# Two attention layers of one kernel: value products in groups of four blocks in the first, and two late units written one head pair earlier in the second

## What is computed

```python
# layer 0, for each of 16 heads; k and v are repeated over 4 heads
s1 = einsum(q1, k1) * scale + mask;  s2 = einsum(q2, k2) * scale + mask
out = einsum(softmax(s1) - lam * softmax(s2), v)         # then a norm over (tokens, 2*DH), and @ Wo
y = mxfp4(input) @ mxfp4(weight).T + bias
# layer 1, for each of 16 heads
attn = softmax(where(causal, q @ k.T / sqrt(16), -inf));  out = attn @ v;  x = out @ Wo + bo
# experts: sigmoid gate, 4 of 16 experts by groups, and one shared expert
```

## Time and profile before

| | |
|---|---|
| median of 3 runs | 812.24 us (810.98 to 812.34) |
| the profiled execution's own time | 813.73 us |
| its span | 812.0 us |
| PE busy | 761.3 us (94%) |
| DVE busy | 552.4 us (68%) |
| ACT busy | 429.8 us (53%) |
| POOL busy | 367.3 us (45%) |
| value products L771, both layers | 216 us in two forms (162.7 and 53.3) |
| mean granted PE clock | 0.985 of 2.4 GHz |

### The profile page before, as it was taken

The page is one execution under the profiler, slowest core; times in us unless marked ns, Lnnn a source line. Parts: engine busy times, 40 slices in busy tenths (PEclk is TensorE's granted clock), DMA queues, the critical chain, the costliest instruction groups (busy, mean ns, idle before and its releaser), DMA issues. The chain is left out here.

```text
span 812.0 us, 12974 instructions
## 1 busy us (share of the span) xinstructions
PE 761.3 (94%) x3783; PEld 370.6 (46%) x3783; DVE 552.4 (68%) x1408; ACT 429.8 (53%) x922; POOL 367.3 (45%) x706
## 2 busy tenths in 40 slices
PE   4888999999999999998998998999799999999995
PEld 3342222222222322224744232332278888888883
DVE  3778777877777777714874886885077665566666
ACT  2432466666656666673242365776745554455552
POOL 1762565664324433431331132335366665566664
PEclk9999899999999999999999999999999999999998
DMA  6394640020011002101056236453442211122111
GB/s 198 125 285 132 148 114 20 18 66 15 15 45 45 16 16 55 35 22 53 1 174 141 79 92 179 155 175 112 144 102 65 65 65 50 55 64 63 66 69 56
DMA packets 56980, 68.86 MB, mean 85 GB/s; under 512 B 13793, under 2 KB 35714, under 8 KB 56915
## 3 DMA queue, kind: packets, MB, share of 16 engines
q1 hardware_dynamic: 56840, 68.10, 29.2%
q10 hardware_dynamic: 80, 0.07, 0.0%
HBM read 46.37 MB, written 15.44 MB: 76 GB/s over the span
## 5 line engine op out<-in xcount | busy, mean ns | idle before, releaser
L823 ACT ACTIVATE top<-ps 128x512 f32<-128x512 f32 (+3 forms) x384 | 170.7, 491 | 126.7 <-PE ps L751 126.7
L751 PE MATMUL ps<-mid 99*128 99x512 bf16 (+3 forms) x576 | 182.9, 333 | 5.7 <-ACT mid L823 3.4
L865 DVE CUSTOM_DVE_ANT_0 ps<-ps,keep 128x512 f32<-128x512 f32 (+3 forms) x320 | 162.0, 530 | 27.3 <-PE ps L727 27.1
L727 PE MATMUL ps<-mid 96*128 96x512 bf16 (+3 forms) x512 | 167.6, 340 | 5.1 <-PEq L249 1.0
L771 PE MATMUL ps<-top,mid 128*33 128x512 f32 (+3 forms) x768 | 162.7, 503 | 0.0
L1652 PE MATMUL ps<-xp,wp 128*128 128x512 f32 (+1 forms) x600 | 146.3, 394 | 3.2 <-ACT wp L1702 2.7
L751 PEld LDWEIGHTS ps<-mid 99*128 99x128 bf16 x576 | 53.7, 98 | 174.9 <-ACT top L823 103.2
L1652 PEld LDWEIGHTS ps<-xp,wp 128*128 128x128 f32 (+1 forms) x600 | 112.7, 188 | 28.6 <-ACT xp L1704 3.2
L960 POOL TENSOR_SCALAR_AFFINE_SELECT top<-top 128x128 f32<-128x128 f32 x256 | 71.2, 291 | 107.3 <-ACT top L823 105.2
L823 ACT ACTIVATE mid<-ps 128x512 f32<-128x512 f32 (+1 forms) x192 | 82.2, 494 | 58.2 <-PE ps L751 36.0
L869 DVE TENSOR_REDUCE top<-ps 128x1 f32<-128x512 f32 x128 | 88.4, 690 | 32.9 <-PE ps L727 32.6
(11 more groups left out here) (217 smaller groups left out, 851.2 us busy)
## 6 DMA issues: line engine op xcount, KB each, us to landing
mid<-part_scratch SPq DMA_DIRECT2D x9, 1152.0 KB, 8.9
part_scratch<-top SPq DMA_DIRECT2D x18, 384.0 KB, 2.9
cw_s<-combine_rows SPq DMA_DIRECT2D x48, 128.0 KB, 3.0
part_scratch<-top SPq DMA_DIRECT2D x18, 256.0 KB, 3.1
top<-in_w SPq DMA_DIRECT2D x6, 634.0 KB, 5.2
mid<-part_scratch SPq DMA_DIRECT2D x9, 384.0 KB, 4.0
top<-in_w SPq DMA_DIRECT2D x4, 640.0 KB, 7.1
top<-in_w SPq DMA_DIRECT2D x4, 633.0 KB, 6.0
```

The lines of the kernel that those rows point to most:

```text
L727: nc.tensor.matmul(ps[:, s_bank(turn), 0:w], queries(pair, m)[0:PARTS, i * P:(i + 1) * P], keys(pair, m)[0:PARTS, c * 512:c * 512 + w], st ...
L751: nc.tensor.matmul(ps[:, ST_BANK + n % AHEAD, 0:w], keys(pair, m)[0:STACK, j * P:(j + 1) * P], queries(pair, m)[0:STACK, q0:q0 + w], start ...
L823: nc.scalar.activation(pr[:, n % RING, 0:w], ps[:, ST_BANK + n % AHEAD, 0:w], ACT.Exp, scale=0.25).then_inc(p_ready, 1)
L865: ins = nc.vector.tensor_tensor_reduce(bank, bank, msk[:, 512 - w:512], -1.0 if low else 1.0, 3e38 if low else -3e38, ALU.add, ALU.min if ...
```

## The change

```diff
-                RING, LAG = 8, 1
-
-                GROUPS = [(b, b + 2) for b in range(0, 8 if not first else PAIR, 2)]
-                if not first:
-                    GROUPS += [(b, b + 4) for b in range(8, PAIR, 4)]
+                RING, LAG = 9 if first else 8, 1
+
+                GROUPS = [(b, b + 2) for b in range(0, 8, 2)] if not first else [(0, 4), (4, 8)]
+                GROUPS += [(b, b + 4) for b in range(8, PAIR, 4)]
...
                             outputs(sp, pair, 0)
-                            if pair == 1:
-                                unsent(sp, 1)
                             if pair + 1 < N:
                                 late(sp, pair + 1)
+                            if pair == 0:
+                                unsent(sp, 1)
```

## The result

The changed kernel takes 814.16 us (median of 13 runs, 812.72 to 817.44); the kernel before, run between them on the same chip, 812.45 us (13 runs, 810.81 to 813.25). The ratio is 1.0033, 95% interval 1.0022 to 1.0044: 1.8 to 3.6 us slower. The forecast was 813.5 us, within 809.5 to 817, and "within 0.2%" was its likeliest case; the interval of the ratio lies just beyond that.

A forecast was written before the change was run, and what follows sets the result against it. PE's own stream was taken as layer 0's bound. Layer 0: -0.5 - 0.2 + 2.9 = +2.2 us; layer 1: -3.4 + 2.5 = -0.9; sum +1.3, so 812.24 becomes 813.5 us, range 809.5 to 817.

The forecast's parts named there:

- The price of a group and a joint: PE, layer 0 value products: a group costs 0.23 us besides its columns, a joint 0.01 to 0.02; each group saved, 0.21.
- Rival 4: Layer 0: weight loads of joints are exposed, four in about 0.15 us; up to +14 us, 826; chance 0.02.
- The stalls: Layer 0: PE waits 0.36 at k = 13, 0.21 at 5, 0.32 at 21, 0.16 at 1; 1.07 of 1.27 us a pair.
- Rival 2: Layer 0: the groups save their whole 19.7 us and nothing stalls, 791.6; chance 0.05.
- The tail: Layer 0's last 38 blocks: stalls of 5.0 us against ten joints worth 2.1, so 2.9 us lost.
- The body of layer 0: Pairs 1 to 13 of layer 0: joints save slightly more than stalls cost, -0.5 us in all, between -2.6 and +1.
- the failed step: Layer 1: moved writes hold SP until some 481, so `rows(2)` is issued late; 2.5 us of stall ending pair 1.
- The other half of the step: Layer 1: PE has no margin for `rows(2)`, so its 2.5 us of lateness become 2.5 us of stall.
- in time but lands behind the writes, 0.3 to 0.8: Layer 1: if SP isn't held, `rows(2)` is issued in time but lands behind the writes, 0.3 to 0.8 us.
- The -3.4 for the two waits: Layer 1: with the writes a pair earlier, PE's waits for near maps (2.3) and `rows(3)` (1.1) go, -3.4 us.
- rival 1: Layer 1: `rows(2)` isn't late, so the whole sum is -0.7 us, 811.5; chance 0.20.
- Rival 3: Layer 0: DVE bounds each run of four, 0.1 us more in each of 3 x 15 turns, +4.5, 818; chance 0.20.

The follow-up runs named there:

- e4: Kernel before plus the moved writes, groups of four only at k = 9, 17 and 1, twos elsewhere and in the tail, eight tiles; 802.83 us, ratio 0.9885.
- e8: Changed kernel with layer 0's group at k = 21 (blocks 16 to 19) split into two groups of two; 810.87 us, ratio 0.9986.
- e6: Changed kernel with ACT's copies of the sums in layer 0 one block later (k = 14 and 6); 813.88 us, ratio 1.0029.
- e10: Changed kernel with ACT's copies one block later and, in layer 0's pairs 4, 8, 12, next rows sent ahead of the inverses' reads; 810.45 us, ratio 0.9985.
- e5: Changed kernel with eight instead of nine tiles in layer 0's ring of exponentials; 820.17 us, ratio 1.0096.
- e3: Changed kernel with groups of two in the last 38 blocks of layer 0; 811.76 us, ratio 0.9994.
- e1: Kernel before with only the change's groups and ring of nine, the writes left in pair 1; 817.07 us, ratio 1.0062.
- e12: Changed kernel with layer 1's `rows(2)` issued behind the output transfers of pair 1 instead of ahead; 816.9 us, ratio 1.0053.
- e2_writes: Kernel before with only the writes of f = 1 moved to pair 0 of layer 1, groups and ring as before; 808.42 us, ratio 0.9947.

## Why the prediction was right in its sum, and where it wasn't

**The price of a group and a joint: right.** 0.21 us a join was forecast. The changed kernel has 1.84 us for a group of four, and 18.5 us less busy time in layer 0 for 94 groups (162.7 to 144.2), 0.20 each; e4 has 18.03 us a pair with three joins; and in e8 one group more and the stall of 0.32 less leave 18.20 of 18.32. The rule of the Trainium skill ("TensorE: Matmul & The Clock Gate", Part 3, The mechanism), by which only another row group lets a weight load overlap, would have made the group of four longer by some loads; it shows 1.91 us with the modelled overlap, where two groups of 1.05 would have had 2.10. The measurement decides: in groups of two column strips with the same 128 rows no load shows. The same section of the Trainium skill also lets a load for the background weight buffer be pulled ahead; whether that is what happens here the trace doesn't tell. Rival 4 is out.

**The stalls: right in place and size.** k = 13: 0.36 forecast, 0.39 in the trace. k = 5: 0.21 and 0.23. k = 1: 0.16 and 0.18. k = 21: 0.32 and 0.31; where DVE has the combination of two maps, PE waits near there for 0.48, one block earlier, ahead of the first score. Three of these in PE's timeline after the change, k = 21, then k = 1 and 5; each wait is the distance of two rows less the columns of the first (0.22 for 512, 0.11 for 256):

```profile
113.26 0.39 PE L750 MATMUL ps<-mid 99*128 99x512 bf16 x1
113.79 0.23 PE L726 MATMUL ps<-mid 96*128 96x128 bf16 x1
...
264.67 0.27 PE L750 MATMUL ps<-mid 99*128 99x256 bf16 x1
264.96 0.28 PE L726 MATMUL ps<-mid 96*128 96x256 bf16 x1
...
266.57 0.38 PE L726 MATMUL ps<-mid 96*128 96x512 bf16 x1
267.02 0.39 PE L750 MATMUL ps<-mid 99*128 99x512 bf16 x1
```

e6 and e10 took ACT's copy from in front of the exponential and gained the 0.2 that the lags gave for it, e8 removed the stall at k = 21 with its join, and e5 lengthened the pairs by what one tile fewer gives. Rival 2, the whole 19.7 us, is out by these stalls; the prediction had set it aside by the row.

**The tail: right.** +2.9 forecast, +2.97 in the trace, and e3 won it back.

**The body of layer 0: sized wrong.** Forecast -0.5 for thirteen pairs, measured +0.67 for twelve. Undisturbed pairs are 18.32 us for a forecast of 18.27, which is 0.6 over twelve; seven of the twelve, those with DVE's extra steps, are 0.20 to 0.25 longer, as forecast, though it had eleven of fourteen. The term that the sum left at nothing is the landing of the rows: the first scores of pairs 5, 9 and 13 wait 0.3, 0.2 and 1.1 us more than before. Not all of that is lost, since PE would have waited for DVE or ACT soon after: the intervals show 0.07, 0 and 0.78 us, 0.85 in all. The prediction asked of every stall what is late next on ACT and DVE, and not on the queues: between the transpose at k = 13 and the first score of the next pair at k = 21 two groups fewer of overhead lay, so SP's transfer had 0.4 us less, and its margin had been next to nothing: before the change the first score of pair 5 stood 0.39 us behind the one ahead where all others had 0.29. Layer 0 came out at +3.8 in the trace for +2.2, inside its bounds of +0.2 to +4; by e1's ratio it is +5.0 (3.1 to 7.1).

**Layer 1: the failed step.** "If the writes hold SP until the gathers are through ... `rows(2)` ... comes 2.5 us late." The writes didn't hold SP: 3.70 us for six, behind gathers, and `rows(2)` was issued at its old place. The row at 52.53 us, three writes in 4.37 us, was taken as the nearest and wasn't; what held SP there no run here shows. The other half of the step, that there is no margin for a late `rows(2)`, was right (at most 0.2 us, e12). The branch that the prediction named and didn't take, "in time but lands behind the writes, 0.3 to 0.8", is what most traces show: 0.2 to 0.8 us in seven of ten, next to nothing in three, the profiled execution of the changed kernel among them. The -3.4 for the two waits came: 18.87 to 15.50 us for pair 2. So layer 1 gives -2.6 to -3.4 and not -0.9, rival 1's case for this half (-2.9), which had 0.20.

So the time was met by two errors that cancel, 1.6 to 2.8 us too little lost in layer 0 and 1.7 to 2.5 too little won in layer 1. That is luck: had only one of the two been sized right, the sum would have moved by that much. Rival 3 (DVE later by 0.1 in each turn) is out: undisturbed pairs lie 0.05 above the forecast, where it had 0.3. What stays open is how the 1.4 us by which the median lies above the profiled execution are made up. Three things differ from trace to trace: the waits for rows in layer 0 (at pair 13 the first score stood 0.99 to 1.55 us behind the one ahead in four traces with all the joins), the landing of `rows(2)`, and the stretches at the lower clock. The unprofiled runs show none of them.

## What to carry to other kernels

Price a join by what it removes and, separately, what it uncovers: walk the engine that bounds from the end of a group to its next need with measured lags, and join only where it arrives later than what it waits for. Here three joins a pair gave about 5 us where six, with the tail, lost 4 to 5. The idle time of the feeding engine summed over a stretch doesn't show it: it was 90 us before and 87 after, and one tile fewer in the ring still cost 0.37 us a pair. And when a stretch between a transfer's issue and its use gets shorter, the transfer belongs on the list of what is late next.

## What the runs showed of the hardware

- Behind an idle stretch of PE of about 2 us came 3.4 us at 1.2 GHz in two traces: behind the wait that ended at 316.46 (e6, clock 0.50 from 317.3), and behind the one that ended at 490.78 (e12, from 492.1). With the clock these waits of 1.8 and 2.2 us cost 2.9 and 3.8 us. It doesn't always follow: in the kernel before PE stood still for 2.3 us until 498.04, and in e1_groups for some 1.9 and 1.7 us until 499.90 and 507.50, and the clock stayed at 2.4 GHz behind all three. Which of the two happens no run here settles. The kernel before, columns as in the earlier trace rows:

```profile
496.00:498.00 2.00, 0.00 (x0) 0.00 (x0) 0.39 (x3) 0.74 (x2) 0.87 (x4) 1.00 1.08 239
498.00:500.00 2.00, 1.96 (x17) 0.84 (x17) 1.12 (x2) 1.09 (x2) 0.00 (x0) 1.00 1.06 220
500.00:502.00 2.00, 2.00 (x13) 0.63 (x9) 1.23 (x6) 1.52 (x4) 0.58 (x2) 1.00 1.06 227
```

- Stretches at the lower clock around 46, 83 and 463 us come and go between executions of nearly the same code (at 83 us 6.8 us of it before and after, 3.4 in e2_writes, none in e4_three_joins; at 463 there before, not after). 3.4 us of it cost 0.9 to 1.3 us of time.
- Six writes of SP behind 1.5 MB of gathers were issued in 3.60 to 4.21 us in the eleven traces that have them there, about as fast as without them (4.05). What changed was their landing: 8.4 to 9.7 us after the issue in the changed kernel, 2.7 to 3.4 before.
- From the issue of `rows(2)` in layer 1 to PE's start on them 2.92 us passed in e12, where PE waited for them and the writes were landing or landed, and 3.56 to 3.88 us in the four traces where PE shows a wait for them behind the writes. In layer 0 at pair 13, behind the reads of the inverses, it was 4.35 to 5.48 us in six traces with all the joins (e5, e1, after, e12, e3, e6).
